# Last layer of a six-layer transformer kernel: the third batch's attention ahead of the fourth's, and its feed forward among the fourth's attention and norm

## The chip, the cores and the metric

The kernel runs on one core of one Trainium2 chip. The metric is the time of one execution on the device, in microseconds (us). TensorE (PE in the profile), VectorE (DVE), ScalarE (ACT), GpSimd (POOL) and SyncE (SP, which starts the DMAs) each work through a list of their own in a fixed order, and wait for each other on semaphores.

## What is computed

Four gated pairs of cross attention and feed forward come first; the change leaves them alone. It is about the last part, a stack of DEPTH = 6 layers of windowed self attention and gated feed forward over B = 4 batches of 512 tokens of width 256:

```python
def attn_layer(x, Wqkv, qs, ksc, Wo):
    qkv = x @ Wqkv
    ...                         # 16 heads of 64, q and k normalized, scaled and rotated
    out = local_attention(q, k, v)    # windows of 64 tokens, each sees itself and the one before
    return out @ Wo

def ffn_layer(x, g, bln, W1, b1, W2, b2):
    mu = x.mean(-1, keepdims=True)
    var = ((x - mu) ** 2).mean(-1, keepdims=True)
    xn = (x - mu) / jnp.sqrt(var + 1e-05) * g + bln
    hg = xn @ W1 + b1
    a, gate = jnp.split(hg, 2, -1)
    return a * jax.nn.gelu(gate, approximate=False) @ W2 + b2

for i in range(DEPTH):
    x = attn_layer(shift_tokens(x), Wqkv[i], q_scale[i], k_scale[i], Wo[i]) + x
    x = ffn_layer(shift_tokens(x), ln_g[i], ln_b[i], W1[i], b1[i], W2[i], b2[i]) + x
return x
```

## The kernel before

`last_order` writes one order of work for all engines: a table from a step number to the parts put there. Each engine walks the table and carries out what is its own in each part, so the table fixes every engine's list. A layer d starts at step 64 d. Steps are given below within the last layer (d = 5): 0 to 63 are those in which new queries and keys are made, and the tail goes on to step 88.

Attention is worked on in units (g, b), a group g of four heads of batch b, and each unit in four tiles of 128 tokens, one tile a step. A tile passes through `qkv` (step t, 12 matmuls of L1493; rotary products on VectorE, L1631 to L1633), `rot` (t+1: squares' sums on VectorE, a power on GpSimd), `tr` (t+3, L1501), `sc` (t+4: scores, L1511 and L1516; row maxima on VectorE, L1645), `ex` (t+4: four exponentials on ScalarE, L1760), `dv` (t+5, L1654 and L1656), `pt` (t+6, L1525; copied by ScalarE, L1766) and `pv` (t+7, L1535; `att_hi` by ScalarE, L1773, `att_lo` by VectorE, L1660). When a unit's four tiles are through, `wo` multiplies by the output matrix (two times 6 matmuls of L1449) and `wx` adds to the tokens on VectorE (L1666). There is one set of score banks, so `sc` of a tile waits until `ex` of the tile before is done. In the second half of the last layer the units run in the order (2,2) (3,2) (3,3) (2,3) (0,2) (1,2) (1,3) (0,3).

The feed forward of a batch has a norm in seven parts: `fo` (GpSimd adds two halves of the tokens, L1826), `fa` (mean by two matmuls, L1553; subtracted on VectorE, L1672), `fq` (squares on ScalarE, L1778; sum on GpSimd, L1829), `fb` (variance by small matmuls, L1558; power on GpSimd, L1832), `fy` (turned by TensorE, L1566; applied on VectorE, L1681), `fc` (bias on ScalarE, L1786) and `fd` (rest on VectorE, L1688). Then come `hg` and `ha`, the two halves of the first matrix in three parts each (66 matmuls of L1449 in all, of 12, 12 and 12 for `hg` and 12, 12 and 6 for `ha`), with the gelu on ScalarE (L1794), and `hm`, which multiplies them (VectorE, L1698), rounds (L1705) and keeps the rests (GpSimd, L1838; VectorE, L1708, for the last tile). `fw` is the second matrix in three parts of 12, 11 and 11 matmuls (L1449, L1593, L1594), `fx` adds its result to the tokens (L1713), and in the last layer `fin` mixes in what was kept (L1719) and sends it out. Each gelu after an exponential, and each exponential after a gelu, makes ScalarE load another table (ACT_TABLE_LOAD).

Weights come in chunks of 512 columns (`lq`): SyncE starts a DMA into one of the two `staged` buffers, VectorE rounds it (L1615), GpSimd makes the rest (L1810). SyncE may start a chunk only when GpSimd has done the chunk before the last; VectorE, in its order, waits for the DMA. The Q, K and V weights of two groups fit at a time.

Batch 2's attention ends at step 59 and batch 3's at step 71. Batch 2's norm is in steps 64 to 71, its first matrix in 72 to 77, its second in 78 to 80; batch 3's norm is in 72 to 78, its feed forward in 79 to 87.

## Time and profile before

| | us |
|---|---|
| median of 3 runs | 4801.31 (4801.25 to 4806.72) |
| the profiled execution, its own time | 4805.08 |
| its span, first to last instruction | 4803.7 |
| PE busy | 4591.3 (96%) |
| DVE busy | 3584.6 (75%) |
| ACT busy | 3135.8 (65%) |
| POOL busy | 2594.6 (54%) |

The busy times are means over very different parts of the program. The last layer's attention ends some 63 us before the end of the span; that stretch and the 100 us ahead of it are where the change lies. Times in the rows below are counted from the start of the span. The trace folds equal instructions that follow each other into one row (x2, x4).

### The profile page before, as it was taken

Reading aid. Unit: us, or ns where it says so; the run is one execution under the profiler, and the core shown is the slowest. Engines: PE = TensorE matmul, PEld = TensorE weight load, DVE = VectorE, ACT = ScalarE, POOL = GpSimd, SP = SyncE. Lnnn points to the kernel's source line nnn. Section 1 sums busy time; section 2 is a strip of 40 time slices with the busy share of each in tenths; the row PEclk is TensorE's granted clock in tenths of the full one; section 3 lists DMA queues with packets and bytes.
Section 4 is the critical chain, followed back from the end, with each engine's and each line's share of the span. In section 5 each row is a group of like instructions: output and inputs, shape, how many; then the busy total and the mean of one; then the engine's idle time right before and its main releaser. Section 6 shows DMA issues by size and latency. Waiting matters only on the chain.

```text
span 4803.7 us, 92378 instructions
## 1 busy us (share of the span) xinstructions
PE 4591.3 (96%) x34598; PEld 2927.6 (61%) x34664; DVE 3584.6 (75%) x6388; ACT 3135.8 (65%) x7744; POOL 2594.6 (54%) x2346
## 2 busy tenths in 40 slices
PE   6999999999999999969999999999999999999998
PEld 2333333334444343337788888888888888888886
DVE  4767766766675857858888887888888888887885
ACT  3666566556455556557777777777777777777773
POOL 3322211212121222148888788787888887887873
PEclk8999999999999999989999999999999999999999
DMA  5323323332222323212111111111111111111110
GB/s 121 66 50 62 75 42 60 71 63 47 57 40 60 68 41 74 40 34 54 41 41 35 41 40 36 42 39 37 39 44 39 39 36 41 40 36 38 39 44 31
DMA packets 178924, 233.05 MB, mean 49 GB/s; under 512 B 29648, under 2 KB 121424, under 8 KB 178256
## 3 DMA queue, kind: packets, MB, share of 16 engines
q1 hardware_dynamic: 178480, 227.14, 21.0%
q8 instruction: 277, 4.54, 0.4%
q14 instruction: 167, 1.37, 0.1%
HBM read 150.09 MB, written 32.51 MB: 38 GB/s over the span
## 4 chain that ended last, share of the span: by engine, by line
PE 66%; DVE 12%; ACT 8%; POOL 7%; issue 5%; DMA 1%; SPq 0%; another core or an unknown queue 0%; DVEq 0%; ACTq 0%; POOLq 0%
PE psum L1449 13%; PE psum L1493 11%; PE psum L541 5%; PE psum L527 5%; PE psum L506 5%; PE psum L1535 3%; PE psum L1501 3%; PE psum L488 2%; DVE maxes L731 2%; PE psum L1516 2%; PE psum L1525 2%; POOL stats L1818 2%; PE psum L530 2%; ACT lprobs L1760 2%; PE psum L496 2%
## 5 line engine op out<-in xcount | busy, mean ns | idle before, releaser
L941 ACT ACTIVATE probs<-psum 128x1024 f32<-128x1024 f32 x610 | 621.6, 1023 | 449.2 <-PE psum L527 259.7
L731 DVE TENSOR_REDUCE maxes<-psum 128x1 f32<-128x1024 f32 x512 | 618.1, 1216 | 278.0 <-PE psum L506 274.2
L1818 POOL TENSOR_TENSOR stats<-stats,minus_half 128x8 f32<-128x8 f32 x384 | 687.6, 1791 | 32.0
L1760 ACT ACTIVATE lprobs<-psum,small_stats,stats 128x128 f32<-128x128 f32 x1536 | 690.3, 480 | 20.9 <-DVE small_stats L1649 19.9
L1493 PE MATMUL psum<-wqkv_hi,xs_hi 128*128 128x512 f32 (+1 forms) x1536 | 546.6, 356 | 16.4 <-POOL xs_lo L1805 15.2
L1814 POOL TENSOR_TENSOR lwork<-lwork 128x512 f32<-128x512 f32 x384 | 505.1, 1315 | 74.7 <-DVE lwork L1633 74.6
L527 PE MATMUL psum<-stack 98*128 98x512 bf16 x1536 | 502.8, 384 | 25.9 <-DVE maxes L731 12.2
L1493 PE MATMUL psum<-wqkv_lo,xs_hi 128*128 128x512 f32 (+1 forms) x1536 | 519.3, 338 | 0.0
L1493 PE MATMUL psum<-wqkv_hi,xs_lo 128*128 128x512 f32 (+1 forms) x1536 | 519.0, 338 | 0.0
L506 PE MATMUL psum<-stack 96*128 96x512 bf16 x1536 | 473.3, 385 | 33.2 <-ACT probs L938 10.0
L728 DVE CUSTOM_DVE_ANT_0 psum<-psum,mask_by_query 128x1024 f32<-128x1024 f32 x256 | 314.8, 1231 | 217.8 <-PE psum L506 216.2
L1741 ACT ACTIVATE lwork<-psum 128x512 f32<-128x512 f32 x384 | 231.4, 603 | 358.0 <-DVE lwork L1633 357.9
L1631 DVE TENSOR_TENSOR lwork<-psum,rotary 128x512 f32<-128x512 f32 x384 | 262.5, 684 | 210.9 <-PE psum L1493 101.9
L541 PE MATMUL psum<-probs,values 128*32 128x512 f32 x3072 | 412.9, 610 | 0.8 <-ACT probs L941 0.8
L1656 DVE TENSOR_TENSOR lprobs<-lprobs,small_stats 128x512 f32<-128x512 f32 x384 | 380.0, 990 | 13.1
L527 PEld LDWEIGHTS psum<-stack 98*128 98x128 bf16 x1536 | 137.8, 100 | 390.0 <-issue 221.7
L1760 ACT ACTIVATION_READ_ACCUMULATOR lprobs<-psum,small_stats,stats 128x1 f32 x1536 | 348.9, 227 | 0.0
L1089 POOL TENSOR_TENSOR attn<-attn,sums 128x512 f32<-128x512 f32 x48 | 62.3, 1298 | 502.5 <-DVE sums L764 502.5
L1493 PEld LDWEIGHTS psum<-wqkv_hi,xs_hi 128*128 128x128 f32 x1536 | 291.4, 190 | 62.1 <-issue 20.9
L1493 PEld LDWEIGHTS psum<-wqkv_lo,xs_hi 128*128 128x128 f32 x1536 | 291.6, 190 | 43.7 <-issue 5.3
L1493 PEld LDWEIGHTS psum<-wqkv_hi,xs_lo 128*128 128x128 f32 x1536 | 290.8, 189 | 32.7
L506 PEld LDWEIGHTS psum<-stack 96*128 96x128 bf16 x1536 | 147.6, 98 | 261.6 <-ACT probs L938 27.8
(244 smaller groups left out, 11398.0 us busy)
## 6 DMA issues: line engine op xcount, KB each, us to landing
mixed_vals<-vals SPq DMA_DIRECT2D x672, 64.0 KB, 2.0
stack<-k_parts SPq DMA_DIRECT2D x288, 128.0 KB
staged<-in_quads SPq DMA_DIRECT2D x144, 256.0 KB, 3.0
k_parts<-parts SPq DMA_DIRECT2D x48, 384.0 KB, 2.9
stack<-q_parts SPq DMA_DIRECT2D x288, 64.0 KB
staged<-in_w SPq DMA_DIRECT2D x54, 256.0 KB, 3.0
ctx<-in_ctxT SPq DMA_DIRECT2D x24, 512.0 KB, 5.2
q_parts<-parts SPq DMA_DIRECT2D x24, 384.0 KB, 3.2
```

The source lines that it names most:

```text
L506: ins = tensor.matmul(ps[:, i, :], q[0:STACK, h, qt * P:(qt + 1) * P], k[0:STACK, h, i * S:(i + 1) * S], start=True, stop=True)
L527: ins = tensor.matmul(ps[:, i, :], ky[0:STACK + 2, h, kt * P:(kt + 1) * P], q[0:STACK + 2, h, :], start=True, stop=L != 1)
L541: ins = tensor.matmul(bank(acc)[32 * h:32 * h + 32, :], values[:, kt, 4 * g + h, :], pr, start=kt == 0, stop=kt == KT - 1)
L728: ins = vector.tensor_tensor_reduce(out=scores, in0=scores, in1=masks_q[:, qt * S2:(qt + 1) * S2], scale=1.0, scalar=-3e38, op0=ALU.add, o ...
L731: ins = vector.tensor_reduce(to, pair(("M", u)), AX.XY, ALU.max)
L941: scalar.activation(probs[:, i % 6, :, :], pair(("E", u)), ACT.Exp).then_inc(S_["E_act"], 1)
L1449: ins = tensor.matmul(ps, l, r, start=first and n == 0, stop=last and n == 2)
L1493: ins = tensor.matmul(to, x_[:, c, b % 2, tok(tt)], w_[:, c * COLS + lo:c * COLS + hi], start=c == 0 and n == 0, stop=c == C - 1 and n == 2)
L1656: vector.tensor_tensor(pr, pr, bc(rc, 2, P), ALU.mult).then_inc(S_["dv_dve"], 1)
L1760: ins = scalar.activation(pr[:, h, :], scores(u)[:, h % 2, h // 2, :], ACT.Exp, bias=st[:, 4 + h:5 + h], scale=y[:, h:h + 1], accum_out=st ...
L1814: gpsimd.tensor_tensor(t1, t1, t2, ALU.add)
L1818: pool_step(gpsimd.tensor_tensor(st[:, 8:16], st[:, 0:8], minus_half[:, :], ALU.pow))
```

## The change

In the last layer only, and from step 35 on:

- The units of the second half run in the order (2,2) (3,2) (0,2) (1,2) (1,3) (0,3) (3,3) (2,3), so that batch 2's attention ends at step 55 and batch 3's at step 71.
- The order needs the weights of groups 3 and 2 twice, so two more sets are loaded (8 more chunks, in steps 52 to 58, 61 and 65), and the second loads of groups 0 and 1 move eight steps ahead, to steps 36 to 49.
- Five of the nine chunks of the feed forward's weights move from steps 35 to 40 to steps 41, 43, 45, 46 and 47. Steps 41 and 45 then have two chunks each.
- Batch 1's last two first-matrix parts and its second matrix move from steps 60 to 69 to steps 57 to 62.
- Batch 2's norm moves from steps 64 to 71 to steps 59 to 63, with `fy`, `fc` and `fd` all in step 63; its first matrix from steps 72 to 77 to steps 64 to 69; its second matrix from 78, 79, 80 to 73, 74, 76, between `fa`, `fb` and `fy` of batch 3's norm, which itself stays in steps 72 to 78.
- For batch 3, `second_matrix` takes the inner tiles 0 to 3 of both halves of the result first, and tiles 4 and 5 of both in the last part. `fx` follows the part that finishes its half.

```diff
 def weights_of(d, g, b):
-    return d, 1 if b >= B // 2 and g < 2 else 0, g
+    again = b >= B // 2 and g < 2 or (d, b) == (DEPTH - 1, B - 1)
+    return d, 1 if again else 0, g
...
-def last_group(b):
-    return 3 - b
+def last_group(d, b):
+    return (3, 2, 1, 2)[b] if d == DEPTH - 1 else 3 - b
+
+def second_matrix(d, b, part):
+    if (d, b) == (DEPTH - 1, B - 1):
+        return [[(0, i) for i in range(4)], [(1, i) for i in range(4)], [(m, i) for m in range(C) for i in (4, 5)]][part]
+    return [(m, i) for m in range(C) for i in range(HT)][4 * part:4 * part + 4]
+
+def done_by(d, b, part):
+    return [m for m in range(C) if (m, HT - 1) in second_matrix(d, b, part)]
...
+    ending = ((2, 2), (3, 2), (0, 2), (1, 2), (1, 3), (0, 3), (3, 3), (2, 3))
...
+        again = (((1, 0), 44, 53), ((1, 1), 48, 57))
+        if d == DEPTH - 1:
+            again = (((1, 0), 36, 45), ((1, 1), 40, 49), ((1, 3), 52, 61), ((1, 2), 56, 65))
...
-        for t, j in ((27, 0), (28, 3), (30, 1), (31, 4), (35, 2), (36, 5), (38, 6), (39, 7), (40, 8)):
+        for t, j in zip((27, 28, 30, 31, 35, 36, 38, 39, 40) if d < DEPTH - 1 else (27, 28, 30, 31, 41, 43, 45, 46, 47), (0, 3, 1, 4, 2, 5, 6, 7, 8)):
...
-            if d == DEPTH - 1 and b == B - 2:
-                gates, linear, second = (40, 42, 44), (41, 43, 45), (46, 47, 48)
+            if d == DEPTH - 1 and b == 1:
+                gates, linear, second = (56, 57, 59), (57, 58, 60), (60, 61, 62)
+            elif d == DEPTH - 1 and b == B - 2:
+                norm, gates, linear, second = (27, 28, 29, 30, 31, 31, 31), (32, 34, 36), (33, 35, 37), (41, 42, 44)
             elif d == DEPTH - 1 and b == B - 1:
                 norm, gates, linear, second = (40, 41, 42, 43, 44, 46, 46), (47, 49, 51), (48, 50, 52), (53, 54, 55)
...
-                put(t0 + t, ("fw", (d, b, i)), *([("fx", (d, b, i - 1))] if i else []))
+                put(t0 + t, ("fw", (d, b, i)), *([("fx", (d, b, j)) for j in done_by(d, b, i)]))
```

The weights' name, the semaphore counts and `last_group` are adapted to it in the engine programs. TensorE has as many instructions as before; VectorE and GpSimd have 8 more of the weight chunks' each, and ScalarE has 4 more table loads (170 for 166). Line numbers of the changed kernel are 19 higher in the engine programs.

VectorE, the part of the list that holds batch 2's `fy` and `fd`. Before, at steps 70 and 71 (`ln_stats` is `fb`, `lwork<-lwork,vecs,psum` is `fy`, `xn_lo` is `fd`, `x_back` is `fin`, `x_resid<-psum,x_resid` is `wx`):

```order
L1676 TENSOR_SCALAR ln_stats<-psum 128x4
L1660 TENSOR_TENSOR att_lo<-psum,att_hi 128x2x128
L1713 SCALAR_TENSOR_TENSOR x_resid<-psum,vecs,x_resid 128x512
L1681 SCALAR_TENSOR_TENSOR lwork<-lwork,vecs,psum 128x512 x2
L1660 TENSOR_TENSOR att_lo<-psum,att_hi 128x2x128
L1719 SCALAR_TENSOR_TENSOR x_back<-x_resid,gates,x_back 128x512 x2
L1666 TENSOR_TENSOR x_resid<-psum,x_resid 128x512 x2
L1688 SCALAR_TENSOR_TENSOR xn_lo<-lwork,vecs,xn_hi 128x512 x2
L1698 SCALAR_TENSOR_TENSOR lwork<-psum,vecs,lwork 128x512 x2
```

With the change, at step 63 and the start of 64 (`lwork<-psum,rotary` is the rotary part of `qkv`, the last row is `sc`):

```order
L1685 TENSOR_TENSOR x_resid<-psum,x_resid 128x512 x2
L1738 SCALAR_TENSOR_TENSOR x_back<-x_resid,gates,x_back 128x512 x2
L1700 SCALAR_TENSOR_TENSOR lwork<-lwork,vecs,psum 128x512 x2
L1707 SCALAR_TENSOR_TENSOR xn_lo<-lwork,vecs,xn_hi 128x512 x2
L1650 TENSOR_TENSOR lwork<-psum,rotary 128x512
L1651 TENSOR_TENSOR lwork<-psum,rotary 128x8x32
L1652 TENSOR_TENSOR lwork<-psum,rotary 128x8x32
L1664 TENSOR_REDUCE psum<-psum 128x4
```

`wx`, `fin`, `fy` and `fd` now stand in one row, with nothing of attention between them, ahead of the rotary products and of the maxima of the next tile's scores.

VectorE, ahead of the last unit's output. Before, the rows above hold it: `att_lo` stands between `fy` and `fin`. With the change, at steps 69 to 71 (the rows between the two `att_lo` are `hm` of batch 2's last tiles):

```order
L1679 TENSOR_TENSOR att_lo<-psum,att_hi 128x2x128
L1717 SCALAR_TENSOR_TENSOR lwork<-psum,vecs,lwork 128x512
L1717 SCALAR_TENSOR_TENSOR lwork<-psum,vecs,lwork 42x512
L1724 CAST hid_hi<-lwork 128x512
L1724 CAST hid_hi<-lwork 42x512
L1727 TENSOR_TENSOR hid_hi<-lwork,hid_hi 42x512
L1679 TENSOR_TENSOR att_lo<-psum,att_hi 128x2x128
L1685 TENSOR_TENSOR x_resid<-psum,x_resid 128x512 x2
```

`hm` of the last tiles has moved ahead of the last `att_lo`, which the output matrix waits for.

TensorE, behind the last product with the output matrix (`wout`). Before (`xn` with `w` is the first matrix of batch 2, L1553 is `fa` of batch 3, L1558 `fb`, L1566 `fy`):

```order
L1449 MATMUL psum<-att_hi,wout_lo 128x512
L1449 MATMUL psum<-xn_hi,w_hi 128x512
...
L1449 MATMUL psum<-xn_hi,w_lo 128x512
L1553 MATMUL psum<-lwork,ones_mean 128x512
L1449 MATMUL psum<-xn_hi,w_hi 128x512
...
L1449 MATMUL psum<-xn_hi,w_lo 128x512
L1558 MATMUL psum<-ones_mean,lwork 128x1 x4
L1449 MATMUL psum<-xn_hi,w_hi 128x512
...
L1449 MATMUL psum<-xn_hi,w_lo 128x512
L1566 MATMUL psum<-ident,ln_stats 128x128 x4
```

With the change (`hid` with `w` is the second matrix of batch 2):

```order
L1468 MATMUL psum<-att_hi,wout_lo 128x512
L1468 MATMUL psum<-hid_hi,w_hi 128x512
...
L1468 MATMUL psum<-hid_hi,w_lo 128x512
L1572 MATMUL psum<-lwork,ones_mean 128x512
L1468 MATMUL psum<-hid_hi,w_hi 128x512
...
L1468 MATMUL psum<-hid_hi,w_lo 128x512
L1577 MATMUL psum<-ones_mean,lwork 128x1 x4
L1468 MATMUL psum<-hid_hi,w_hi 128x512
...
L1613 MATMUL psum<-hid_hi,w_lo 128x512
L1585 MATMUL psum<-ident,ln_stats 128x128 x4
L1468 MATMUL psum<-xn_hi,w_hi 128x512
```

Batch 3's norm stood between parts of the first matrix of batch 2 (24, 24 and 12 matmuls apart), and stands now between parts of the second (12, 11 and 11), with the first matrix of batch 3 straight behind `fy`.

## Rows read from the trace of the kernel before

**Rows 1.** Stretches: length, busy us (count) of PE, PEld, DVE, ACT, POOL; PE clock, DMA, GB/s.

```profile
4100.00:4200.00 100.00, 98.89 (x949) 81.13 (x947) 81.68 (x170) 73.77 (x236) 82.64 (x77) 1.00 0.14 39
...
4680.00:4720.00 40.00, 37.77 (x395) 30.31 (x394) 26.03 (x57) 30.93 (x94) 22.50 (x22) 1.00 0.10 26
4720.00:4760.00 40.00, 31.65 (x180) 24.75 (x181) 19.89 (x34) 12.30 (x26) 8.26 (x7) 0.87 0.09 27
4760.00:4804.00 44.00, 36.87 (x164) 29.29 (x163) 23.13 (x34) 6.62 (x10) 12.19 (x9) 0.96 0.10 36
```

**Rows 2.** TensorE in order of time: start, us, line, operands, count, idle before and releaser.

```profile
4700.92 0.30 PE L1511 MATMUL psum<-band_bias,ident_b 64*64 64x256 bf16 x4
...
4706.00 0.30 PE L1511 MATMUL psum<-band_bias,ident_b 64*64 64x256 bf16 x4
...
4713.25 0.30 PE L1511 MATMUL psum<-band_bias,ident_b 64*64 64x256 bf16 x4 [2.11 <-ACT lprobs L1760]
...
4725.50 0.34 PE L1535 MATMUL psum<-turned,mixed_vals 128*64 128x64 f32 x4 [2.78 <-issue]
...
4737.87 0.50 PE L1449 MATMUL psum<-att_hi,wout_hi 128*128 128x512 f32 x1 [1.44 <-DVE att_lo L1660]
...
4740.49 0.39 PE L1449 MATMUL psum<-att_hi,wout_lo 128*128 128x512 f32 x1
4743.99 0.79 PE L1449 MATMUL psum<-xn_hi,w_hi 128*128 128x512 f32 x1 [3.11 <-DVE xn_lo L1688]
...
4759.77 1.05 PE L1558 MATMUL psum<-ones_mean,lwork 128*128 128x1 f32 x8 [1.02 <-POOL lwork L1829]
...
4793.49 0.50 PE L1449 MATMUL psum<-hid_hi,w_hi 128*128 128x512 f32 x1 [0.65 <-POOL hid_lo L1838]
```

**Rows 3.** Stretches with a lower granted clock, columns as in rows 1.

```profile
4726.00:4730.00 4.00, 4.00 (x19) 3.33 (x17) 1.96 (x4) 1.40 (x3) 1.27 (x1) 0.60 0.02 4
...
4744.00:4747.00 3.00, 3.00 (x7) 2.42 (x8) 0.00 (x0) 0.00 (x0) 0.00 (x0) 0.50 0.57 165
```

**Rows 4.** TensorE, the first matrix of batch 3, first and last matmul of the 54.

```profile
4777.68 0.39 PE L1449 MATMUL psum<-xn_hi,w_hi 128*128 128x512 f32 x1
...
4789.73 0.39 PE L1449 MATMUL psum<-xn_hi,w_lo 128*128 128x512 f32 x1
```

**Rows 5.** VectorE in order of time, columns as in rows 2.

```profile
4618.83 1.28 DVE L1666 TENSOR_TENSOR x_resid<-psum,x_resid 128x512 f32<-128x512 f32 x2
...
4717.13 1.40 DVE L1698 SCALAR_TENSOR_TENSOR lwork<-psum,vecs,lwork 128x512 f32<-128x512 f32 x2 [0.82 <-PE psum L1449]
...
4719.24 1.65 DVE L1708 TENSOR_TENSOR hid_hi<-lwork,hid_hi 42x512 fp32r<-42x512 f32 x1
...
4765.06 1.41 DVE L1681 SCALAR_TENSOR_TENSOR lwork<-lwork,vecs,psum 128x512 f32<-128x512 f32 x2 [4.03 <-PE psum L1566]
...
4770.31 1.42 DVE L1688 SCALAR_TENSOR_TENSOR xn_lo<-lwork,vecs,xn_hi 128x512 fp32r<-128x512 f32 x2
```

**Rows 6.** ScalarE in order of time, columns as in rows 2.

```profile
4706.22 1.28 ACT L1794 ACT_TABLE_LOAD   x1
4707.52 1.39 ACT L1794 ACTIVATE lwork<-psum,vecs 128x512 f32<-128x512 f32 x2
...
4757.23 1.15 ACT L1778 ACTIVATE lwork<-lwork 128x512 f32<-128x512 f32 x2
...
4766.51 1.34 ACT L1786 ACTIVATE xn_hi<-lwork,vecs 128x512 fp32r<-128x512 f32 x2 [1.37 <-DVE lwork L1681]
```

**Rows 7.** GpSimd in order of time: parts of batch 3's norm, columns as in rows 2.

```profile
4741.69 1.70 POOL L1826 TENSOR_TENSOR lwork<-x_resid 128x512 f32<-128x512 f32 x1 [8.75 <-DVE x_resid L1666]
...
4758.45 1.27 POOL L1829 TENSOR_TENSOR lwork<-lwork 128x512 f32<-128x512 f32 x1 [1.45 <-ACT lwork L1778]
...
4763.30 1.01 POOL L1832 TENSOR_TENSOR ln_stats<-ln_stats,minus_half 128x4 f32<-128x4 f32 x1
```

**Rows 8.** The DMAs of weight chunks into `staged`, 4300 to 4804 us.

```profile
DMA to landing us min/median/max: 2.9/3.1/4.5
```

More of the change, by code:

```diff
@@ L1226, in last_order @@
     halves = [((0, 0), (1, 0), (1, 1), (0, 1), (2, 0), (3, 0), (3, 1), (2, 1)), ((2, 2), (3, 2), (3, 3), (2, 3), (0, 2), (1, 2), (1, 3), (0, 3))]
-    units = [(d, g, b) for d in range(DEPTH) for half in halves for g, b in half]
+    ending = ((2, 2), (3, 2), (0, 2), (1, 2), (1, 3), (0, 3), (3, 3), (2, 3))
+    units = [(d, g, b) for d in range(DEPTH) for half in (halves if d < DEPTH - 1 else (halves[0], ending)) for g, b in half]
     for d in range(DEPTH):
         t0 = 64 * d
-        for key, q, o in (((0, 0), -4, 5), ((0, 1), 0, 9), ((0, 2), 12, 21), ((0, 3), 16, 25), ((1, 0), 44, 53), ((1, 1), 48, 57)):
+        again = (((1, 0), 44, 53), ((1, 1), 48, 57))
+        if d == DEPTH - 1:
+            again = (((1, 0), 36, 45), ((1, 1), 40, 49), ((1, 3), 52, 61), ((1, 2), 56, 65))
+        for key, q, o in (((0, 0), -4, 5), ((0, 1), 0, 9), ((0, 2), 12, 21), ((0, 3), 16, 25)) + again:
             load(t0 + q if t0 + q >= 0 else -2, 1 if t0 + q >= 0 else 0, ("q", d) + key, range(3))
             load(t0 + o, 1, ("o", d) + key, range(1))
-        for t, j in ((27, 0), (28, 3), (30, 1), (31, 4), (35, 2), (36, 5), (38, 6), (39, 7), (40, 8)):
+        for t, j in zip((27, 28, 30, 31, 35, 36, 38, 39, 40) if d < DEPTH - 1 else (27, 28, 30, 31, 41, 43, 45, 46, 47), (0, 3, 1, 4, 2, 5, 6, 7, 8)):
             load(t0 + t, 0, ("f", d), [j])
@@ L1342, in banks_taken @@
             if stage == "fw":
-                return [("fw", u[:2], m) for m in range(C) if m == u[2]]
+                return [("fw", u[:2], m) for m in range(C) if (m, 0) in second_matrix(*u)]
             if stage == "wo":
@@ L1581, in tensor_program @@
                     PE.wait_ge(S_["lq_pool"], loaded(("f", d), HT, HT + 1 + (part > 0)))
-                    for m, i in [(m, i) for m in range(C) for i in range(HT)][4 * part:4 * part + 4]:
+                    for m, i in second_matrix(d, b, part):
                         to = bank(("fw", (d, b), m))
@@ L1728, in scalar_program @@
                     if d or b > 1:
-                        A.wait_ge(S_["qkv_pe"], at_("qkv", (d, last_group(b - 2), b - 2, QT - 1) if b > 1 else (d - 1, last_group(b + 2), b + 2, QT - 1)))
+                        A.wait_ge(S_["qkv_pe"], at_("qkv", (d, last_group(d, b - 2), b - 2, QT - 1) if b > 1 else (d - 1, last_group(d - 1, b + 2), b + 2, QT - 1)))
                     for c in range(C):
@@ L1823, in gpsimd_program @@
                     d, b = u
-                    G.wait_ge(S_["add_dve"], at_("wx", (d, last_group(b), b, C - 1)))
+                    G.wait_ge(S_["add_dve"], at_("wx", (d, last_group(d, b), b, C - 1)))
                     left(work_at, ("n0", u), G)
```

## The prediction

> **What bounds the kernel now.** First the stretches of time. Through the layers TensorE is busy 98.89 of 100 us while no other engine passes 83 [rows 1]: it is bound by its own list, and a change can only pay where TensorE idles or runs at a lower clock. That is the end: 2.2 us idle from 4680 to 4720, 8.4 to 4760 and 7.1 to the end, 17.7 together [rows 1], of which the last 4.9 (result, DMA) always stay. Next the list of TensorE in time shows where: 2.11 us in front of the scores of step 66 behind the exponentials, 2.78 in front of a `pv`, 1.44 in front of the last output product, 3.11 in front of batch 2's first matrix, and about a microsecond at two places after it [rows 2]. Third the granted clock: it is 0.60 from 4726 to 4730, behind the 2.78, and 0.50 (1.2 GHz for 2.4) from 4744, behind the 3.11 [rows 3]; there 7 matmuls take 3.0 us, 0.43 each, where 53 steps of batch 3's first matrix take 12.05, 0.227 each [rows 4]. It lasts some 6 us, about 13 matmuls, so it costs 13 x 0.2 = 2.6 us. All told some 17 us of idle time and low clock are there to win. The tail is not free of chains, though: the norm of the last batch is one, of five engines' turns.
>
> **What the change keeps.** TensorE's count of matmuls stays, so the work moved is a zero sum; I place it by stage to see the idle time of each. I measure from three points of before: scores of step 64 at 4700.92, of step 66 at 4713.25, last output product done at 4740.9 (4740.49 and 0.4) [rows 2].
>
> **Steps 56 to 63: +14.1 us.** They gain two parts of batch 1's first matrix (12 + 6) and its second (34), 52 x 0.227 = 11.8 us [rows 4], and the three TensorE parts of batch 2's norm, some 2.3 (`fb` alone 1.05 [rows 2]; two matmuls for `fa`, four transposes for `fy`). That is denser than before, about 8.4 us a step (eight steps of 2.3 and 2.15 for attention, 1.4 for the output, and the batch's share), while VectorE's share of a step is some 4.5 us (80% of a full stretch [rows 1]) plus the `hm` of 2.1 to 3.8 and a norm part. I take no idle time here.
>
> **Steps 64 and 65: +4.9 us.** This is where the change makes a new wait. In step 63 VectorE has, in one row, `wx` 1.28, `fin` 1.4 (two operations of the kind of `fy`), `fy` 1.41, then it waits for `fc` on ScalarE, 1.34, then `fd` 1.42, then the rotary products 1.35 [rows 5, 6]. With the time of the scores of step 62 as 0: TensorE's step 62 takes 9.25 (attention's small parts 2.3, which is step 64's 5.08 less 12 matmuls [rows 2, 4]; `fw` 11 x 0.227 = 2.5; `fb` 0.9; output product 6 x 0.227 = 1.4; `qkv` 2.15, six matmuls of that form and six of half the width). In step 63 `att_lo`, `rot` and `dv` are done at 14.2 (they begin when `pv` has run at 11.9 and ScalarE has copied it), `wx` at 15.5, `fin` at 16.9, `fy` at 18.3, `fc` at 19.7, `fd` at 21.1, rotary at 22.4, maxima of step 64 at 23.3. TensorE begins step 64 at 15.65 and is through its small parts at 17.95; `hg` of batch 2 waits for `fd`: 3.15 us idle. It ends at 23.9, and the scores of step 65 wait for exponentials that could start only at 23.9, behind a square and copies that waited for the rotary: ready at 25.75. So step 64 takes 10.15 us where it took 5.08. Step 65 has 12 matmuls as before and the same two ScalarE table loads around it (gelu 1.28 + 1.39, exponentials' load 1.28 [rows 6]), so it takes 7.1 for 7.25. Sum +4.9. The low clock that a 3.11 us gap brought [rows 3] mostly falls into the 1.85 us that TensorE would wait anyway: **+0.7**. If `fin` and `fd` were hidden, the term would be 0; if each of the three took half a microsecond longer beside a busy GpSimd, 6.
>
> **Steps 66 to 71: -1.1, and +2.5 for the clock.** Now batch 2's first matrix (30 matmuls) stands where batch 1's `ha`, 23 of `fw` and its `fo` to `fy` stood. It fills the 2.78 us gap down to 0.85 (the exponentials of step 67 now need a table load of 1.28 first). But `hm` of the last tiles, 3.76 us on VectorE (4717.13 to 4720.89 [rows 5]), stands ahead of the last `att_lo`, and starts only when `ha` ends in step 69. The last output product waits for it: 3.6 us idle instead of 1.44. Added up from the scores of step 66: 26.5 us instead of 27.65. A gap of that length let the clock fall twice [rows 2, 3], so its following 12 or 13 matmuls cost 2.5 more. Bounds: 0 to 2.6.
>
> **From the last output product: -16.4 us.** Before, 62.8 us remained (4803.7 less 4740.9). With the change the 66 matmuls of batch 2's first matrix are gone from here, and the norm of batch 3 lies bare but for `fw`: 12 `fw` matmuls 2.75 (cover for `wx` 0.7 and `fo` 1.3 to 1.7 [rows 7]), `fa` 0.86, then VectorE 1.28, ScalarE 1.15, GpSimd 1.27 [rows 6, 7] against 11 matmuls of 2.5, so 1.4 idle, `fb` 0.9, 11 matmuls 2.5 (cover for GpSimd's 1.01), `fy` 0.6, then 1.41, 1.34 and 1.42 with nothing on TensorE: its first matrix starts at 15.95, behind 4.45 us of idle time. Then 66 x 0.227 = 15.0, low clock again 2.6. From the end of the first matrix to the end of the program before took 13.7 us (4789.96 to 4803.7), with 0.8 of waiting in front of tile 4 of the second matrix at 4793.49 [rows 2]; the new order puts 24 matmuls (5.5 us) ahead of that tile, which is ready after 3.5, so 12.9. Sum 15.95 + 15.0 + 2.6 + 12.9 = 46.4.
>
> **Weight chunks.** Eight more, each 0.42 on VectorE and 1.3 on GpSimd, lie beside TensorE's work. Steps 41 and 45 have two each, so the chunks at 42 and 46 start when GpSimd frees a buffer one step before, and 3.1 us of landing [rows 8] meets a step of 6 us: I take 0, at most 1 us of VectorE's time each. Moving five chunks later costs nothing, as the first use (step 48) is three steps behind the last of the first matrix's.
>
> **The sum.** 14.1 + 4.9 + 0.7 - 1.1 + 2.5 - 16.4 = +4.7 us on an execution that took 4805.08 by its own time (span 4803.7), so 4809.8; that one lies 3.8 above the median of 4801.31, so 4806.0, or +0.1%. The moved work does fill gaps, but puts two new chains in the way.
>
> **Rivals.** (B) The gain comes through: VectorE gets `fy`, `fc`, `fd` done in the cover of `qkv` and the scores, and the clock doesn't fall at the two new gaps. For: in step 53 and 54 the same parts of batch 1 cost TensorE nothing. Against: there they had a step each. 14.1 - 1.1 - 16.4 = -3.4: 4797.9. (C) Slower beyond the measurement: the paired chunks. VectorE stands in its list until the DMA has landed; if GpSimd, 82% busy [rows 1], frees the buffer less than 3.7 us (landing and start) before VectorE reaches the chunk, the maxima of the next scores wait. At steps 42 and 46, 3 us each with nothing absorbed, +6: 4812. Against: a chunk comes round every 2.4 us at best (3.1 + 0.4 + 1.3 over two buffers), and here there are four in three steps of 6 to 7. (D) Table loads: four more (a gelu between exponentials in steps 65 to 68). They decide if a switch costs more than the load. As a mechanism here: a second 1.28 us of ScalarE for each, on the path, +5.1: 4811. Against: the first gelu starts 0.02 us after the load ends, and the load starts at the end of what is ahead [rows 6].
>
> The Trainium skill, "ScalarE: Activation LUTs", section "What ACT_TABLE_LOAD costs", states that each switch to another set costs the load of some 1283 ns and a drain of about 1380 ns more, 2.66 us. By that rule four switches would be 10.6 us of ScalarE's time instead of 5.1, an estimate from that page, and it speaks against this change. This trace agrees on the load (1.28) and shows no drain beside it.
>
> **How the numbers follow.** Forecast 56%, B 26%, C 10%, D 3%, 5% for something larger on either side. A measurement of this kernel can tell about 0.2% from no change, 9.6 us: faster means below 4791.7, slower above 4810.9. The forecast's own bounds (low clock 0 or 2.6 at each of three places, the chain of step 63 from 0 to 6) run from 4798 to 4811; with B, C and D, 4796 to 4814. Faster 5%, slower 14%, same 81%.
>
> **What would show it.** Right: after the scores of step 64 TensorE idles some 3 us in front of `hg` behind VectorE's `xn_lo`; some 3.6 us in front of the last output product behind `att_lo`; about 1.4 in front of `fb` and 4.5 in front of batch 3's first matrix; last output product to end 46 us, not 63; no wait in front of tile 4. Wrong: no gap before `hg` of batch 2 (B), VectorE idle behind a DMA around steps 42 and 46 and TensorE below 98% there (C), a ScalarE gap beside a table load (D).

## The result, and the profile after

| | before | changed |
|---|---|---|
| median of 18 runs each, on one chip, us | 4803.98 (4800.2 to 4806.72) | 4811.26 (4808.56 to 4818.02) |
| ratio of the times | | 1.0017 [1.001, 1.0024] |
| the profiled execution, its own time | 4805.08 | 4809.73 |
| its span | 4803.7 | 4808.4 |

The changed kernel takes 7.3 us more by the medians and 4.7 more by the two spans. The ratio lies under the 0.2% named ahead, and its interval reaches past it. The totals of the page have hardly moved:

```profile
PE 4592.4 (96%) x34664; PEld 2925.7 (61%) x34664; DVE 3585.6 (75%) x6396; ACT 3141.3 (65%) x7748; POOL 2603.2 (54%) x2354
```

TensorE has the same 34664 matmuls and one microsecond more of busy time. So the 4.7 us must be looked for in idle time and in its clock, stretch by stretch (changed kernel, columns as in [rows 1]):

```profile
4640.00:4680.00 40.00, 37.55 (x341) 29.93 (x333) 29.27 (x61) 27.59 (x80) 30.73 (x28) 1.00 0.19 55
4680.00:4720.00 40.00, 37.86 (x353) 31.18 (x351) 29.94 (x57) 24.88 (x74) 24.80 (x24) 1.00 0.16 45
4720.00:4760.00 40.00, 31.99 (x270) 24.85 (x271) 25.50 (x48) 25.76 (x67) 12.62 (x10) 0.94 0.07 23
4760.00:4809.00 49.00, 37.56 (x154) 29.69 (x152) 18.72 (x30) 6.39 (x10) 10.30 (x8) 0.88 0.10 32
```

TensorE idles 2.1, 8.0 and 11.4 us in the last three, 21.6 together, where it idled 17.7 [rows 1]. And it idles 2.45 in a stretch in which the kernel before idled 0.56 (39.44 of 40 busy); that stretch lies ahead of everything that the forecast put a wait into. In the list of TensorE in order of time the idle ahead of a row stands in brackets, with its releaser:

```profile
4645.95 0.38 PE L1512 MATMUL psum<-wqkv_hi,xs_hi 128*128 128x256 f32 x1 [0.85 <-DVE att_lo L1679]
4647.62 0.30 PE L1530 MATMUL psum<-band_bias,ident_b 64*64 64x256 bf16 x4 [0.69 <-ACT lprobs L1779]
...
4715.48 0.30 PE L1530 MATMUL psum<-band_bias,ident_b 64*64 64x256 bf16 x4
...
4721.36 0.79 PE L1468 MATMUL psum<-xn_hi,w_hi 128*128 128x512 f32 x1 [3.50 <-DVE xn_lo L1707]
...
4733.11 0.30 PE L1530 MATMUL psum<-band_bias,ident_b 64*64 64x256 bf16 x4 [2.00 <-ACT lprobs L1779]
...
4757.64 0.50 PE L1468 MATMUL psum<-att_hi,wout_hi 128*128 128x512 f32 x1 [3.74 <-DVE att_lo L1679]
...
4769.76 1.05 PE L1577 MATMUL psum<-ones_mean,lwork 128*128 128x1 f32 x8 [1.35 <-POOL lwork L1848]
...
4778.41 0.79 PE L1468 MATMUL psum<-xn_hi,w_hi 128*128 128x512 f32 x1 [4.54 <-DVE xn_lo L1707]
...
4795.30 0.39 PE L1468 MATMUL psum<-xn_hi,w_lo 128*128 128x512 f32 x1
...
4803.05 0.40 PE L1613 MATMUL psum<-hid_hi,w_lo 106*128 106x512 f32 x1
```

L1530 are the scores of steps 56, 64 and 66. The gap of 2.00 ahead of step 66 stood there before as well (2.11 [rows 2]). The other four large gaps, 3.50, 3.74, 1.35 and 4.54, are the ones that were forecast (the 1.35 for 1.02 before [rows 2]): `hg` of batch 2 behind `xn_lo`, the last output product behind `att_lo`, `fb` and the first matrix of batch 3. The first two rows are a gap that nobody had forecast. What went on ahead of it is seen on VectorE:

```profile
4638.27 1.40 DVE L1738 SCALAR_TENSOR_TENSOR x_back<-x_resid,gates,x_back 128x512 f32<-128x512 f32 x2
...
4644.34 0.43 DVE L1634 CAST wqkv_hi<-staged 128x512 fp32r<-128x512 f32 x1 [3.40 <-DMA staged<-in_quads]
```

and on SyncE, which issues the transfers (same columns):

```profile
4639.03 1.01 SPq L1894 DMA_DIRECT2D out_xT<-x_back  x2
4640.09 0.46 SPq L1878 DMA_DIRECT2D staged<-in_quads  x1
```

SyncE takes its list in order too. In step 54 `fin` of batch 0 stands ahead of one of the added weight chunks. It waits for VectorE's `x_back` (L1738), so the chunk's transfer starts at 4640.09 and not when its buffer is free; VectorE reaches the chunk's rounding at 4640.9 and stands for 3.40 us. The maxima of step 55's scores and everything behind them wait with it.

The granted clock (the third column from the right) was low at three places:

```profile
4721.00:4725.00 4.00, 3.64 (x9) 2.93 (x10) 3.80 (x10) 2.40 (x10) 1.59 (x3) 0.57 0.63 209
4759.00:4763.00 4.00, 4.00 (x12) 3.19 (x11) 1.38 (x2) 0.00 (x0) 0.04 (x1) 0.60 0.00 0
4778.00:4783.00 5.00, 4.59 (x11) 3.65 (x12) 0.35 (x1) 0.00 (x0) 0.00 (x0) 0.53 0.42 122
```

What it costs I read as busy time times what is missing from 1.00 in the granted clock: 3.64 x 0.43 + 4.00 x 0.40 + 4.59 x 0.47 = 5.3 us. By slices of 1 us from 4700 on it is 5.4, and 4.5 before. "Low clock" with a number below is always this sum by slices. It says how much less TensorE could do in that time, and not how much later the program ends: part of it can fall into time in which TensorE would have waited.

With the scores of a tile and the end of the last output product as marks (4740.9 before, 4762.15 changed), the 4.7 us fall to these stages:

| stage | forecast | trace |
|---|---|---|
| ahead of step 36 (same code) | 0 | -1.4 |
| steps 36 to 54 | 0 | -0.2 |
| step 55 | 0 | +1.7 |
| steps 56 to 63 | +14.1 | +14.5 |
| steps 64 and 65 | +5.6 | +5.3 |
| step 66 to the last output product | +1.4 | +1.4 |
| from there to the end | -16.4 | -16.6 |

### The profile page after: what moved, and what is told of

Read it like the earlier page. It is cut to its first block, busy times and chain, and to the rows that moved or that the text cites. A ratio compares the mean times of both kernels' runs of the same rounds, so it can differ in the third digit from the quotient of the medians.

```text
span 4808.4 us, 92474 instructions
## 1 busy us (share of the span) xinstructions
PE 4592.4 (96%) x34664; PEld 2925.7 (61%) x34664; DVE 3585.6 (75%) x6396; ACT 3141.3 (65%) x7748; POOL 2603.2 (54%) x2354
## 3 DMA queue, kind: packets, MB, share of 16 engines
q8 instruction: 277, 4.54, 0.4%
## 4 chain that ended last, share of the span: by engine, by line
PE 67%; DVE 12%; ACT 8%; POOL 7%; issue 5%; DMA 1%; SPq 0%; DVEq 0%; ACTq 0%; POOLq 0%
PE psum L1468 13%; PE psum L1512 11%; PE psum L541 5%; PE psum L527 5%; PE psum L506 5%; PE psum L1554 3%; PE psum L1520 3%; PE psum L488 2%; PE psum L1544 2%; DVE maxes L731 2%; PE psum L1535 2%; PE psum L530 2%; POOL stats L1837 2%; PE psum L496 2%; ACT lprobs L1779 1%
## 5 line engine op out<-in xcount | busy, mean ns | idle before, releaser
L731 DVE TENSOR_REDUCE maxes<-psum 128x1 f32<-128x1024 f32 x512 | 618.1, 1216 | 276.9 <-PE psum L506 273.2
L1779 ACT ACTIVATE lprobs<-psum,small_stats,stats 128x128 f32<-128x128 f32 x1536 | 690.3, 480 | 22.5 <-DVE small_stats L1668 21.6
L1512 PE MATMUL psum<-wqkv_hi,xs_hi 128*128 128x512 f32 (+1 forms) x1536 | 546.2, 356 | 18.3 <-POOL xs_lo L1824 16.4
```

What stands on the lines that cost most here:

```text
L731: ins = vector.tensor_reduce(to, pair(("M", u)), AX.XY, ALU.max)
L1512: ins = tensor.matmul(to, x_[:, c, b % 2, tok(tt)], w_[:, c * COLS + lo:c * COLS + hi], start=c == 0 and n == 0, stop=c == C - 1 and n == 2)
L1779: ins = scalar.activation(pr[:, h, :], scores(u)[:, h % 2, h // 2, :], ACT.Exp, bias=st[:, 4 + h:5 + h], scale=y[:, h:h + 1], accum_out=st ...
```

## The experiments

Each edit is to the changed kernel where nothing else is said; steps are those of the last layer. "From step 40" is the time from the scores of step 40 to the end of the span, which leaves out what the unchanged part does: 266.0 before, 272.2 changed. Where one time is given, the kernel ran once; the changed kernel's own 18 times lie between 4808.56 and 4818.02, so such a time says little, and the steps are compared instead. Every kernel but the changed one was profiled once.

**The chunk ahead of `fin`.** Only SyncE's and VectorE's place of `fin` within step 54 moves.

```
             return 40 if p[0] not in rank else rank[p[0]]
+        if p == ("fin", 0):
+            return 33
         return 31
```

> The changed kernel with one part moved: the result of batch 0 (fin) stands behind the weight chunk of step 54 instead of ahead of it. Theory: in the changed kernel SyncE starts that chunk only after it has waited for VectorE's fin and sent the result out, and VectorE waits 3.40 us for the chunk; step 55 takes 7.88 us and step 56 8.40. With the chunk first, the wait is gone, step 55 takes 6.2 and step 56 about 7.6: 2.2 to 2.5 us less from step 54 to 57. Rival: the 3.40 us are GpSimd's backlog (it frees the buffer late), then both steps stay as they are.

SyncE now issues the chunk 5 us before the output:

```profile
4635.55 0.58 SPq L1880 DMA_DIRECT2D staged<-in_quads  x1
4640.57 1.65 SPq L1896 DMA_DIRECT2D out_xT<-x_back  x2
```

and VectorE doesn't wait for it:

```profile
4639.47 0.41 DVE L1636 CAST wqkv_hi<-staged 128x512 fp32r<-128x512 f32 x1
```

Step 55 takes 6.18 (7.88), step 56 takes 7.56 (8.40), the numbers of the kernel before: 2.5 us, and the gaps of 0.85 and 0.69 are gone. The cause is shown. But the whole took 4809.11 (span 4807.8), and from step 40 it is 271.6, only 0.6 less. The other large gaps are nearly the same (3.49, 3.74, 1.36, 4.32). What differs is the clock, low at four places instead of three:

```profile
4718.00:4725.00 7.00, 6.28 (x32) 4.60 (x32) 4.50 (x11) 5.00 (x15) 4.07 (x4) 0.52 0.39 123
4755.00:4759.00 4.00, 3.98 (x11) 3.16 (x12) 0.69 (x1) 0.00 (x0) 0.00 (x0) 0.57 0.00 0
4769.00:4773.00 4.00, 3.85 (x12) 2.79 (x11) 0.82 (x2) 0.00 (x0) 0.47 (x1) 0.57 0.00 0
4777.00:4783.00 6.00, 5.83 (x14) 4.62 (x15) 0.11 (x1) 0.31 (x1) 0.00 (x0) 0.52 0.34 103
```

That is 9.2 us of low clock for 5.4. Of the 3.8 more, 1.5 fell into steps 64 and 65 and cost nothing: together they take 17.62 us for 17.63, as the gap ahead of the scores of step 66 shrank from 2.00 to 0.90. The rest stands behind step 66, from which to the end it is 77.3 us for 75.3. That this clock comes from the edit is not shown: the kernel with the chunks one at a time (below) has the same edit, low clock of 5.5 and 269.8 from step 40, so there 2.3 of the 2.5 us arrive at the end.

**`hm` of batch 2's last tiles a step later**, in step 70 instead of 69, behind the last `att_lo`.

```
-                put(t0 + linear[j], ("ha", (d, b, j)), ("hm", (d, b, j)))
+                put(t0 + linear[j], ("ha", (d, b, j)))
+                put(t0 + (38 if (d, b, j) == (DEPTH - 1, 2, 2) else linear[j]), ("hm", (d, b, j)))
```

> The changed kernel with hm of batch 2's last tiles moved from step 69 to 70, behind the last att_lo. Theory: the 3.74 us in front of the last output product are VectorE's 3.76 us of hm; they shrink to about 1, and the clock doesn't fall there (2.5 us more). hm then holds up the addition behind the last output product and so the norm of batch 3 by about 1.1. From the scores of step 66 to the end: 5.0 less 1.1, about 4 us less. Rival: the wait only moves on to the norm, and less than 2 us come back.

```profile
4754.39 0.50 PE L1469 MATMUL psum<-att_hi,wout_hi 128*128 128x512 f32 x1 [0.94 <-DVE att_lo L1680]
```

The gap of 3.74 is 0.94: the prediction named the right instruction. But of the 4 us that were expected to the end less than half came, as the rival had it. Time 4805.87. From the scores of step 66 to the end it is 73.5 us for 75.3: 1.8 came back of 2.8. A gap of 0.6 appears ahead of `fa`, and the clock fell behind the 1.99 us gap (step 66 takes 7.98 for 6.43) and not behind the 3.49 ahead of `hg`. Step 64 takes 10.50 all the same, as in the changed kernel with its low clock there, and 1.06 of waiting stands ahead of the scores of step 65 instead. All low clock: 3.9.

**`fin` of batch 1 later**, in step 66 instead of 63.

```
-                put(t0 + second[2] + 1, ("fin", b))
+                put(t0 + (66 if b == 1 else second[2] + 1), ("fin", b))
```

> The changed kernel with batch 1's fin moved from step 63 to 66. Theory: it is 1.4 us of the chain in front of hg of batch 2; the 3.50 us gap there shrinks to 2.1 and the scores of step 65 come 1.4 us earlier: step 64 takes 9.1 us instead of 10.50. The lower clock behind the gap may go too, which is worth up to 0.7. Rival: the time is set by ScalarE's list (squares and table loads), and step 64 stays above 10.

Step 64 takes 8.82 for 10.50 and the gap ahead of `hg` is 1.81 for 3.50: the two `fin` operations (1.4 us in the row at step 54) were in that chain in full, and 0.3 more. Time 4808.2; low clock 7.0 for 5.4, and from step 40 on 273.2. The move as such worked, and in this execution nothing of it arrived at the end.

**Batch 2's norm earlier as well**: `fin` as above, and `fq`, `fb` and `fy` a step earlier.

```
-                norm, gates, linear, second = (27, 28, 29, 30, 31, 31, 31), (32, 34, 36), (33, 35, 37), (41, 42, 44)
+                norm, gates, linear, second = (27, 28, 28, 29, 30, 31, 31), (32, 34, 36), (33, 35, 37), (41, 42, 44)
```

> The changed kernel with batch 1's fin in step 66 and batch 2's norm as in the run with all three moves (fq in 60, fb 61, fy 62), and nothing else. Theory: on top of fin alone (step 64 at 8.82 us, gap 1.81) the earlier fy takes the 1.4 us of VectorE out of the chain and leaves a gap of 0.69 in front of hg of batch 2, step 64 at 7.7; step 61 takes 0.9 more, as fb there has less ahead of it. Rival: the gain of step 64 in the run with all three came from the chunk of step 54, then step 64 stays at 8.8.

```profile
4718.55 0.50 PE L1468 MATMUL psum<-xn_hi,w_hi 128*128 128x512 f32 x1 [0.69 <-DVE xn_lo L1707]
```

Step 64 takes 7.69, with 0.69 left of the gap, and 1.08 stands ahead of the scores of step 65. Steps 61 to 63 together take 22.8 for 22.6, so the earlier norm costs 0.2 there. Time 4808.9, low clock 6.0.

**All three together.** The first, the second and the fourth edit in one kernel.

> The changed kernel with all three moves at once (the chunk of step 54 ahead of fin, hm behind the last att_lo, batch 1's fin to step 66) and with batch 2's fq a step earlier, fb in step 61 and fy in step 62, so that fc and fd alone stay in step 63. Theory: three chains on VectorE and SyncE cost the change 2.2, 4 and 5 us, so 11 us less than the changed kernel, 4 us below the kernel before: ratio to it 0.999. Rival: the stages are too dense for the other engines whatever their order, the waits move to the next engine, and less than half, 5 us, comes back: ratio 1.000 or above.

```profile
4770.28 0.80 PE L1471 MATMUL psum<-xn_hi,w_hi 128*128 128x512 f32 x1 [4.54 <-DVE xn_lo L1710]
```

The gaps ahead of `hg` and of the last output product are 0.69 and 0.94, as in the kernels with one edit; this one stays. 4802.64 (11 runs), 1.0001 [0.9992, 1.001] against the kernel before; from step 40 265.5, 6.6 less than changed, where 11 were expected. So the three waits together weigh as much as the whole difference between the change and the kernel before, and no more: the ratio of 0.999 did not come. One by one they are 2.5, 2.8 and 2.8 us, 8.1 together; 1.08 ahead of the scores of step 65 and 0.62 ahead of `fa` stand as waits now, and the clock still falls twice, 4.4 us.

**Cover for the bare norm.** To the three, the last part of batch 2's second matrix moves from step 76 to 77, behind `fy` of batch 3, and batch 2's `fin` to step 81.

```
-                norm, gates, linear, second = (27, 28, 28, 29, 30, 31, 31), (32, 34, 36), (33, 35, 37), (41, 42, 44)
+                norm, gates, linear, second = (27, 28, 28, 29, 30, 31, 31), (32, 34, 36), (33, 35, 37), (41, 42, 45)
```

> The kernel with all three moves, and the third part of batch 2's second matrix (11 matmuls, 2.5 us) from step 76 to 77, behind fy of batch 3, with batch 2's fin at step 81. Theory: the gap of 4.54 us in front of batch 3's first matrix, which costs itself and about 2.6 us of low clock, becomes a gap of 1.2 in front of fy and one of about 2.2 in front of the first matrix: 1.1 us less idle time, and if the clock stays up 2.6 more, so 1 to 4 us less than with the three moves. Rival: any gap of 2 us lets the clock fall all the same, then 1 us.

```profile
4765.66 0.65 PE L1588 MATMUL psum<-ident,ln_stats 128*128 128x128 f32 x4 [1.35 <-POOL ln_stats L1854]
...
4772.57 0.50 PE L1471 MATMUL psum<-xn_hi,w_hi 128*128 128x512 f32 x1 [2.16 <-DVE xn_lo L1710]
```

4801.82, ratio 0.9997 [0.9987, 1.0006]: no difference to the kernel before, and 0.0004 of the ratio from the kernel above, less than a measurement tells. From step 40 it is 265.1 for 265.5. The 4.54 became 1.35 and 2.16, so 1.0 less, and the clock fell behind them all the same (5.0 us for 4.4), as the rival had it. Moving eleven matmuls within the chain bought no more than that.

**The first matrix behind the exponentials.** In the kernel with the chunk ahead of `fin`, batch 1's second matrix (it needs nothing of ScalarE) takes the steps 64 to 66 among the last exponentials, and batch 2's first matrix is kept from step 68 on as cover for batch 3's norm.

```
-                gates, linear, second = (56, 57, 59), (57, 58, 60), (60, 61, 62)
+                gates, linear, second = (56, 57, 59), (57, 58, 60), (64, 65, 66)
-                norm, gates, linear, second = (27, 28, 29, 30, 31, 31, 31), (32, 34, 36), (33, 35, 37), (41, 42, 44)
+                norm, gates, linear, second = (27, 28, 28, 29, 30, 31, 31), (36, 40, 43), (37, 40, 43), (44, 45, 46)
...
+            products, added, finish = linear, second, second[2] + 1
+            if d == DEPTH - 1 and b == 1:
+                finish = 69
+            elif d == DEPTH - 1 and b == B - 2:
+                products, added, finish = (39, 42, 44), (44, 45, 47), 49
```

`products` are the steps of `hm`, `added` those of `fx`, `finish` that of `fin`, for batches 1 and 2.

> The changed order of units and weights, with the chunk of step 54 ahead of fin, but with batch 1's second matrix in steps 64 to 66 (34 matmuls that need nothing of ScalarE), batch 2's first matrix from step 68 on (hg and ha in 68 and 69, 72 twice, 75 twice), its second in 76 to 78, and hm and fx placed behind what the norm of batch 3 waits for. Theory: what the change lost is where it put the first matrix of batch 2: between exponentials, and away from the bare norm. Steps 64 and 65 then take 5 each (10.50 and 7.13 changed), the gaps of 3.74 and 4.54 shrink to 1 each, and the clock falls once at most: 12 us less than the changed kernel from the scores of step 64 on and 2.5 before, some 8 below the kernel before, ratio 0.998. Rival: the order of units itself costs the time (more weights, denser steps 56 to 63), then it stays at or above the kernel before.

```profile
4694.30 1.86 PE L1586 MATMUL psum<-ones_mean,lwork 128*128 128x1 f32 x8 [2.92 <-POOL lwork L1857]
...
4739.02 0.48 PE L1563 MATMUL psum<-turned,mixed_vals 128*64 128x64 f32 x4 [2.23 <-ACT turned L1794]
...
4767.33 1.05 PE L1586 MATMUL psum<-ones_mean,lwork 128*128 128x1 f32 x8 [2.84 <-POOL lwork L1857]
```

4804.39, ratio 1.0003 [0.9995, 1.0012], where 0.998 was expected; from the scores of step 64 to the end it is 93.2 us for 92.9 changed, and not 12 less. The gaps of 3.50, 3.74 and 4.54 are gone, and new ones of 2.92, 2.55 (ahead of the scores of step 65), 2.23 and 2.84 stand for them. The first is batch 2's norm, of which `fa` and `fq` share step 60, now 6.66 us for 9.39; the last is `fb` of batch 3, whose sum on GpSimd (L1857, 1.26 us, from 4766.02) stands behind `hid_lo` of 2.62 us, put there by `hm` of step 74. This expectation failed by these waits and not by the new order as such, as the kernel with everything covered shows.

**The chunks one at a time.** The fifth and seventh chunk of the feed forward's weights, in steps 41 and 45, go to 39 and 44; `fin` as in the first experiment.

```
-        for t, j in zip((27, 28, 30, 31, 35, 36, 38, 39, 40) if d < DEPTH - 1 else (27, 28, 30, 31, 41, 43, 45, 46, 47), (0, 3, 1, 4, 2, 5, 6, 7, 8)):
+        for t, j in zip((27, 28, 30, 31, 35, 36, 38, 39, 40) if d < DEPTH - 1 else (27, 28, 30, 31, 39, 43, 44, 46, 47), (0, 3, 1, 4, 2, 5, 6, 7, 8)):
```

> The changed kernel with the chunk of step 54 ahead of fin, and with five feed forward chunks at steps 39, 43, 44, 46 and 47, so that no step has two. Theory: two chunks in a step cost TensorE 0.25 us at steps 42 and 46 each, through VectorE, and no more: both steps return to 5.80 from 6.06 and 6.05, 0.5 us together. Rival: the 8 further chunks cost by their number, not by their pairing, and both steps stay.

Steps 42 and 46 take 6.12 and 6.10; 6.06 and 6.05 with the change, 5.80 before. So taking the pair apart brings nothing back. Why is seen on VectorE, from its rounding of the hidden values to the row maxima of step 46's scores (L1645, L1666), which the exponentials wait for. In the kernel before:

```profile
4578.07 0.83 DVE L1705 CAST hid_hi<-lwork 128x512 fp32r<-128x512 f32 x2
...
4580.09 1.48 DVE L1615 CAST wqkv_hi<-staged 128x512 fp32r<-128x512 f32 x1
4581.49 0.69 DVE L1645 TENSOR_REDUCE psum<-psum 128x4 f32<-128x512 f32 x1
```

and with the chunks one at a time:

```profile
4577.80 1.14 DVE L1726 CAST hid_hi<-lwork 128x512 fp32r<-128x512 f32 x2
...
4580.13 1.48 DVE L1636 CAST wout_hi<-staged 128x512 fp32r<-128x512 f32 x1
4581.53 0.69 DVE L1666 TENSOR_REDUCE psum<-psum 128x4 f32<-128x512 f32 x1
```

The maxima start 2.86 us after the scores before, 3.12 with the change and 3.17 here, and the step takes 5.80, 6.05 and 6.10: it grows with that start. Changed, the second chunk's rounding (0.42, and 0.34 to the next instruction) is what is new ahead of them, so the pair does bring the 0.25. Here it is gone, but `hid_hi` takes 1.14 for the 0.75 of the changed kernel and eats it up; step 42 shows the same (1.16 for 0.77). Why `hid_hi` is longer stays open. The stretched rounding of 1.48 (below) can't be the cause in step 46, for the kernel before has it too.

**The new order of the last matrix alone**, in the kernel before: only `second_matrix` for batch 3.

```
+    if (d, b) == (DEPTH - 1, B - 1):
+        return [[(0, i) for i in range(4)], [(1, i) for i in range(4)], [(m, i) for m in range(C) for i in (4, 5)]][part]
+    return [(m, i) for m in range(C) for i in range(HT)][4 * part:4 * part + 4]
```

> The kernel before with one part of the change alone: the last batch's second matrix takes tiles 0 to 3 of both halves of the result first. Theory: the gap in front of tile 4 (0.65 us and what lies around it) goes, the last product ends 0.8 us earlier after the end of the first matrix: 12.9 us from there to the end of the program instead of 13.7. Rival: the first half's addition no longer lies beside the second half's products and comes back at the end, then 13.7.

```profile
4787.79 0.39 PE L1461 MATMUL psum<-xn_hi,w_lo 128*128 128x512 f32 x1
...
4795.54 0.40 PE L1606 MATMUL psum<-hid_hi,w_lo 106*128 106x512 f32 x1
```

From the last matmul of the first matrix to the last of all it takes 7.75 us, as it does with the change (4795.30 to 4803.05), for 8.70 before; the gap of 0.65 [rows 2] is gone. So 0.9 us of the change is this part's, the one part that was run alone in the kernel before. From step 40 it is 266.9 for 266.0, with low clock 6.2 for 4.5. Whole time 4802.16, too little apart to be told.

**Everything covered.** The kernel with the first matrix behind the exponentials, mended at the waits that it showed: one part of batch 2's norm a step, `hm` a step later, behind the `fq` that GpSimd's `hid_lo` had stood ahead of, and batch 1's second matrix spread.

```
-                gates, linear, second = (56, 57, 59), (57, 58, 60), (64, 65, 66)
+                gates, linear, second = (56, 57, 59), (57, 58, 60), (64, 65, 67)
-                norm, gates, linear, second = (27, 28, 28, 29, 30, 31, 31), (36, 40, 43), (37, 40, 43), (44, 45, 46)
+                norm, gates, linear, second = (27, 28, 29, 30, 31, 32, 33), (36, 40, 43), (37, 40, 43), (44, 45, 46)
-                products, added, finish = (39, 42, 44), (44, 45, 47), 49
+                products, added, finish = (40, 43, 44), (44, 45, 47), 49
```

> The arrangement of the run with batch 2's first matrix behind the attention, mended at the five waits that its trace shows: batch 2's norm spread again over steps 59 to 65 (fb 62, fy 63, fc 64, fd 65; it cost gaps of 2.92 and 2.55 us), batch 1's second matrix in steps 64, 65 and 67 (the last part covers 2.23 in front of pv), hm of batch 2 in steps 72, 75 and 76, so that GpSimd does fo and fq of batch 3 first (0.94 and 2.84). Theory: the order of units is harmless, the waits are what the placing of the norms and of hm makes; without them 11 us of gaps and 3 of low clock go: 12 to 14 us less than that arrangement, ratio to the kernel before 0.9975. Rival: a chain taken away gives way to the next (exponentials, VectorE), and the ratio stays at 0.999 or above.

4794.56 (11 runs, 4792.94 to 4796.77) against 4803.41 (15 runs) on the same chip: **0.9979 [0.997, 0.9988]**, by 0.2% faster than the kernel before. It is 9.8 us less than the kernel with the first matrix behind the exponentials, on the same chip too, where 12 to 14 were expected. All gaps of 0.5 us or more ahead of TensorE's work from step 54 to the end of attention's last output:

```profile
4696.46 0.30 PE L1539 MATMUL psum<-band_bias,ident_b 64*64 64x256 bf16 x4 [1.76 <-ACT lprobs L1788]
...
4718.76 0.30 PE L1539 MATMUL psum<-band_bias,ident_b 64*64 64x256 bf16 x4 [0.88 <-ACT lprobs L1788]
...
4728.21 0.30 PE L1539 MATMUL psum<-band_bias,ident_b 64*64 64x256 bf16 x4 [0.61 <-ACT lprobs L1788]
...
4743.76 0.50 PE L1477 MATMUL psum<-att_hi,wout_hi 128*128 128x512 f32 x1 [0.94 <-DVE att_lo L1688]
```

and one of 0.65 in the second matrix. By stretches, the low clock last:

```profile
4720.00:4760.00 40.00, 38.39 (x282) 29.92 (x279) 22.70 (x45) 18.05 (x51) 9.88 (x9) 1.00 0.09 27
...
4697.00:4705.00 8.00, 8.00 (x53) 7.21 (x46) 4.82 (x11) 4.84 (x17) 7.09 (x8) 0.57 0.07 18
```

1.6 us idle from 4720 to 4760 where the change had 8.0, and low clock at one place, 8.00 x 0.43 = 3.4 us for 5.4 (it begins ahead of 4700, so here the sum does too). From step 40 to the end it is 258.1 for 272.2.

**The changed kernel once more**, for what of it repeats.

> The changed kernel itself, profiled once more. Theory: the gaps are the order's and come back within 0.1 us (0.85 and 0.69 in step 55 and 56, 3.50, 2.00, 0.85, 3.74, 1.35, 4.54), while the places and the length of low clock move by some us between executions of one program, as they did between kernels that differ only elsewhere (3.9 to 9.2 us lost). Rival: the low clock follows from the code, then it is the same to 0.5 us, 5.4 lost.

```profile
4721.00:4725.00 4.00, 4.00 (x11) 3.14 (x12) 3.63 (x9) 2.91 (x12) 2.11 (x3) 0.57 0.64 204
4757.00:4763.00 6.00, 5.86 (x15) 4.71 (x16) 1.21 (x3) 0.00 (x0) 0.00 (x0) 0.56 0.00 0
4779.00:4783.00 4.00, 4.00 (x12) 3.09 (x12) 0.00 (x0) 0.00 (x0) 0.00 (x0) 0.57 0.41 115
```

4809.65. The gaps are 3.49, 2.00, 0.85, 3.74, 1.36 and 4.53: each within 0.02 us of the first trace. The low clock comes at the same three places and ends there at the same times, but by slices of 1 us its second stay begins 3 us earlier and its third 3 us later, 6.0 us lost for 5.4 (part of both differences lies in idle time, which the rows above leave out). So the gaps are the order's, while how long a stay at the low clock lasts differs between executions of one kernel. The sums differ by little more than the 0.5 us of the rival, and two executions don't show that 3.9 and 9.2 can come from one kernel.

## Why the prediction was right

The forecast was 4806.0 within 4796 to 4814, and +4.7 us. Measured were 4811.26, within the range, and +4.7 by the spans, +7.3 by the medians. Of the 5.3 us between 4806.0 and 4811.26, 2.7 are the kernel before, whose median came as 4803.98 with 18 runs for 4801.31 with 3. That the spans agree to a tenth is luck in part: the stages from step 36 on add up to +6.1, and the unchanged code ahead of them ran 1.4 faster.

- **Steps 56 to 63, +14.1 (measured +14.5).** Right; TensorE was full, busy for 66.94 of the 67.86 us. Of the 14.5, 0.85 is step 56, still held up by the chunk, so the moved work itself took 13.7.
- **Steps 64 and 65, +5.6 (+5.3).** Right in mechanism and size: `xn_lo` came 3.50 us late where 3.15 was worked out, step 64 took 10.50 for 10.15 and step 65 7.13 for 7.1. That `wx`, `fin`, `fy`, `fc` and `fd` in a row were the chain is shown by the kernels that take links out: without `fin` 1.81, with the norm earlier as well 0.69.
- **Steps 66 to 71, -1.1 and +2.5 (+1.4).** Right in the mechanism: 3.74 idle ahead of the last output product for a forecast of 3.6, and moving `hm` alone takes 2.8 of it away. The `pv` gap went from 2.78 to 0.85 as said. That the sum came out is luck: the low clock took 1.6 of the 2.5, and work and waits 0.9 more than added up.
- **From the last output product, -16.4 (-16.6).** Right, with 1.35 and 4.54 for 1.4 and 4.5. The 12.9 behind the first matrix is confirmed by the kernel with only this order (12.7, and 12.7 with the change).
- **Weight chunks, 0 (2.5, in steps 55 and 56).** This step failed. It looked at the buffers and at VectorE, for steps 42 and 46, and did not follow the third queue that the eight added chunks pass, SyncE's. There the chunk of step 54 stands behind `fin`, which waits for VectorE. The form was rival C's, VectorE standing for a DMA, at another place and for another reason, and at less than half its price. Steps 42 and 46 took 0.25 us more each besides, by the second chunk's rounding ahead of the maxima; step 52 took 0.9 less.
- **Rival B** (the gain comes through) fell, since both new gaps came. And with those waits taken out the change comes to 4802.64, level with the kernel before and not 3.4 below it; the 4.54 us of waiting behind the bare norm of batch 3 stay. **Rival D** (a drain beside each table load) fell. The four added loads cost 1.28 us each, and the gelu follows at once in the tail too (ScalarE, changed kernel):

```profile
4738.09 1.28 ACT L1813 ACT_TABLE_LOAD   x1
4739.38 1.27 ACT L1813 ACTIVATE lwork<-psum,vecs 128x512 f32<-128x512 f32 x2
```

- **The clock** was taken at +0.7, +2.5 and +2.6. The granted clock took 1.6, 1.6 and 2.2 us there, and the first of them cost nothing: step 64 takes 10.50 with it and without (`hm` a step later). So all three terms were too large, by 0.7, 0.9 and 0.4, and the waits and the work beside them too small by most of that. A fixed price for each gap does not hold: with gaps nearly alike, 5.4, 6.0 and 9.2 us were lost. The median's 2.6 us beyond the spans' difference no run explains.

What went wrong with the change itself is answered by the two kernels that keep batch 2's first matrix for the end: not the new sequence of units, since the fastest kernel has it, but what was put where. In the fastest kernel, work that needs nothing of ScalarE stands among the last exponentials, and the 66 matmuls of the first matrix stand beside the last norm. Which of its moves brings how much is not shown, and whether the new sequence of units brings anything is not either: the old sequence with work placed this way was not run.

## What to carry to other kernels

When work is moved to fill gaps, follow each in-order queue it passes, the one that only starts transfers too, and ask what in front of the moved part waits for another engine. In a tail, place the parts of a chain one a step and keep the largest block of independent matmuls beside the last chain that has none; count the idle time before you count the moves. Judge a single removed wait by the stretch it stood in, and the end of the kernel only together with the low clock of the same execution: the same 2.5 us showed there as 0.6 in one kernel and as 2.3 in another.
